# Penalties applied to every self-attention tile by GpSimd, two heads at a time, in a decoder layer

## The chip, the cores and the metric

The kernel runs on one core of a Trainium2 chip. The metric is the device time of one execution in microseconds (us); three executions of the kernel before took 903.59, 895.02 and 897.58 us, median 897.58. The engines are PE (TensorE, matrix products), DVE (VectorE), ACT (ScalarE), POOL (GpSimd) and SP, which issues most of the DMAs. Each engine works through its own list of instructions in order; semaphores tie the lists together.

## The reference, cut to what matters

Four batches of 512 positions with 256 features pass through gated self-attention, cross-attention (both 16 heads of 16 dimensions), and a quantised feed-forward block, each with a residual and a LayerNorm.

```
g = sigmoid(x @ Wg + bg);  Zi = g (row), Zj = g (column)
res   = (1-Zi)*max(1-Zi-Zj, 0) + Zi*min(1-Zi+Zj, 1)
scope = clip((s-2)**(1-g) + 2 - |i-j|, 1e-32, 1)
log_pen = log(max(res*scope, 1e-32))           # 512 x 512 per batch, the same for all heads
scores  = q k^T / 4 + log_pen                  # self-attention
probs   = softmax(scores);  ctx = probs @ v
cross:  probs = softmax(q k^T / 4 + mask * -1e9)
```

Adding log_pen ahead of the exponential is the same as multiplying the exponential by the penalty. A softmax allows any shift per row, as long as nothing overflows or vanishes.

## The kernel before, in words

The attention part is cut into 32 groups of four heads: 16 self groups (4 batches x 4), 16 cross groups. In order: self 0; self 1, cross 0; self 2, cross 1; self 3, cross 2; cross 3, with four groups each, numbered 0 to 31 (self groups are 0 to 7, 12 to 15 and 20 to 23). A group has 16 tiles of 128 x 512 scores.

A **step** has 16 slots and works on three groups at once. In slot i of step n, PE makes the score tile i+2 of group n for its row maxima (`max_tile`, L1400, rows are queries) and the transposed score tile i of group n-2 for its exponentials (`exp_tile`, L1420, rows are keys); DVE takes a row maximum (`row_max`, L921); ACT takes an exponential (`exponential`, L813); and PE multiplies finished probabilities with V (`context`, L1445), four heads per instruction group, in two halves per key tile. "s1,2" below is the step whose maxima are those of self-attention of batch 1, group 2; "c" is cross. The maxima become an extra set of rows of the query stack: DVE splits them in three bf16 parts (`shift_part`, L905 to L911, slots 0 and 1), PE turns them (`m`, slot 5), ACT copies and stores them; the product with them then subtracts the maximum. At the step's end all this moves on by one group.

Between these, slots carry **jobs** from a table written by hand (`make_plan`): projections `q`, `k` (PE L1303, two copies on ACT L726, then on POOL `rest` L655, on ACT `middle` L732, on POOL `low` L660), `v`, the gates (`gate`, `gates`, `diagonals`, `reach`), the penalties (`pen`, DVE, seven instructions for each of four 128 x 512 tiles, L978 to L990), residual and LayerNorm jobs, output projection, and the weights of the feed-forward (`wprep`). DVE runs the jobs of a slot two slots late (`DVE_LAG`), POOL one slot late (`POOL_LAG`).

How far one engine may run ahead is set by buffers: two PSUM banks for maxima, three for exponentials, two for jobs, and `NP` = 8 probability tiles. In slot i, `max_tile` waits until the maximum two tiles back is taken, and `exp_tile` until the exponential three tiles back is done. What stands behind a waiting instruction on its engine waits too.

**Penalties before.** ACT makes the logarithm of all four penalty tiles (`ln`, L756, which changes ACT's function table twice). DVE's row maximum adds it (`lp`) to the scores. For the transposed tiles there are two ways by key tile (kt). For kt 1 and 3 the logarithm is turned by PE and kept in two f16 parts, and PE adds both to the scores by products with an identity (L1424, L1425). For kt 0 and 2 (`MUL_KT`) the penalty itself is turned, and POOL multiplies the exponentials of each head with it (`multiply`, L645, 128 x 512 each).

The context of a key tile is computed in the next key tile's slots (`i % GH >= 2`, kt = i // GH - 1); the last one falls into the next step (slots 1, 2).

## Time and profile before

| | |
|---|---|
| times of three runs | 903.59, 895.02, 897.58 us |
| profiled execution | its span is 894.6 us; the page gives no other time for it |
| busy | PE 714.0, DVE 655.1, ACT 483.9, POOL 290.8 us |
| steps with exponentials of self groups | 93.5 to 300.9, 382.0 to 482.2 and 561.4 to 665.2 us |
| last context of the attention | 795.8 us; the feed-forward follows |

The profile shows for each instruction when it ran and what ended the engine's idle time before it. A DVE or POOL instruction that is held up after it was started is shown longer, not as idle: the duration holds the wait. A matmul's duration holds the passage through the array, so its cost in a dense row is read from the distance of two starts. The limits of a step are taken where ACT copies the context of its group (L792), so "the step of group n" runs from the copy of group n-1 to that of group n.

### The profile page before, as it was taken

The page shows a single profiled execution, that of the slowest core. Times are in us where ns is not written, and L with a number is a line of the kernel's source. Part 1 is how long each engine was busy: PE and PEld are TensorE (multiplying, and loading weights), DVE is VectorE, ACT ScalarE, POOL GpSimd, SP SyncE. Part 2 cuts the span into 40 slices and gives each one's busy share as a digit, 9 for nine tenths or more (in the row PEclk, how much of TensorE's full clock was granted, in tenths as well). Part 3 has the DMA queues.
Part 4 walks back from the last instruction along what each step waited for, and adds up shares of the span by engine and source line. Part 5 has one row for each costly group of instructions (what it writes and reads, how often), then busy time and mean ns, then how long its engine had stood idle before and what let it go on. Part 6 is the DMA issues. An engine that isn't in the chain of part 4 may idle for free.

```text
span 894.6 us, 12845 instructions
## 1 busy us (share of the span) xinstructions
PE 714.0 (80%) x4374; PEld 281.8 (31%) x4374; DVE 655.1 (73%) x1704; ACT 483.9 (54%) x800; POOL 290.8 (33%) x257
## 2 busy tenths in 40 slices
PE   5156878998778889999898899997788699974754
PEld 3033222443223233444232333442222134332221
DVE  5956794676589777688995666689787477717996
ACT  2312446554445767745456677445456476863634
POOL 4202554544445313235463022455223000001314
PEclk9587899999889999999899999999899799996965
DMA  2662111110221313302222123134111411000002
GB/s 69 172 169 86 38 56 56 56 50 14 73 62 56 92 38 103 88 18 62 61 57 77 52 59 93 42 86 111 56 37 39 100 51 32 6 1 1 0 1 94
DMA packets 34896, 54.00 MB, mean 60 GB/s; under 512 B 4368, under 2 KB 25872, under 8 KB 34832
## 3 DMA queue, kind: packets, MB, share of 16 engines
q1 hardware_dynamic: 32912, 51.61, 20.1%
q10 hardware_dynamic: 1920, 1.57, 1.1%
q8 instruction: 36, 0.59, 0.3%
q14 instruction: 28, 0.23, 0.1%
HBM read 36.91 MB, written 14.68 MB: 58 GB/s over the span
## 4 chain that ended last, share of the span: by engine, by line
PE 43%; DVE 28%; ACT 8%; POOL 7%; issue 6%; DMA 4%; SPq 3%; ACTq 0%; POOLq 0%; DVEq 0%
PE ps L1445 9%; DVE unused L921 9%; PE ps L1400 8%; PE ps L1420 6%; PE ps L1387 5%; PE ps L1303 4%; POOL probs L645 3%; PE ps L1380 2%; ACT probs L813 2%; PE ps L1424 2%; PE ps L1425 2%; DMA xT<-in_xT 2%; POOL rest L655 2%; DMA KS<-parts_kc 2%; DVE x L958 1%
## 5 line engine op out<-in xcount | busy, mean ns | idle before, releaser
L1400 PE MATMUL ps<-KS,QS 96*128 96x512 bf16 x512 | 205.1, 402 | 91.4 <-DVE mx L921 62.2
L813 ACT ACTIVATE probs<-ps 128x512 f32<-128x512 f32 x256 | 149.3, 596 | 167.3 <-PE ps L1425 107.7
L645 POOL TENSOR_TENSOR probs<-probs,penT 128x512 f32<-128x512 f32 x128 | 165.4, 1310 | 205.4 <-ACT probs L813 205.2
L921 DVE CUSTOM_DVE_ANT_0 unused<-ps,lp 128x512 bf16<-128x512 f32 x256 | 171.1, 685 | 77.1 <-PE ps L1400 73.0
L1420 PE MATMUL ps<-QS,KS 108*128 108x512 bf16 x512 | 199.5, 393 | 7.1 <-ACT probs L813 7.0
L813 ACT ACTIVATE probs<-ps,mask_col 128x512 f32<-128x512 f32 x256 | 166.4, 687 | 58.0 <-PE ps L1420 56.6
L921 DVE CUSTOM_DVE_ANT_0 unused<-ps,mask_rest 128x512 bf16<-128x512 f32 x192 | 128.9, 684 | 45.5 <-PE ps L1400 44.1
L1400 PEld LDWEIGHTS ps<-KS,QS 96*128 96x128 bf16 x512 | 50.7, 99 | 242.9 <-DVE mx L921 144.4
L655 POOL TENSOR_TENSOR rest<-proj,parts 128x512 f32<-128x512 f32 x32 | 39.0, 1218 | 169.3 <-ACT parts L726 168.7
L1445 PE MATMUL ps<-probs,v_s 128*32 128x256 f32 x1024 | 84.5, 403 | 5.6 <-POOL probs L645 4.8
L1445 PE MATMUL ps<-probs,v_c 128*32 128x256 f32 x1024 | 82.9, 397 | 0.6 <-ACT probs L813 0.6
L1420 PEld LDWEIGHTS ps<-QS,KS 108*128 108x128 bf16 x512 | 50.6, 100 | 44.6 <-ACT probs L813 18.4
L627 POOL TENSOR_SCALAR rstd<-mv 128x4 f32<-128x4 f32 x12 | 2.7, 225 | 152.9 <-DVE mv L949 152.9
L921 DVE CUSTOM_DVE_ANT_0 unused<-ps,mask_row 128x512 bf16<-128x512 f32 x64 | 43.4, 682 | 12.2 <-PE ps L1400 12.1
L1424 PE MATMUL ps<-lpT_hi,ident_h 128*128 128x512 f16 x128 | 51.6, 403 | 0.0
L1425 PE MATMUL ps<-lpT_lo,ident_h 128*128 128x512 f16 x128 | 51.3, 400 | 0.0
L660 POOL TENSOR_TENSOR parts<-rest,parts 128x512 bf16<-128x512 f32 x32 | 38.5, 1203 | 19.0 <-ACT parts L732 19.0
L921 DVE DVE_READ_ACCUMULATOR2_ANT mx<- 128x1 f32 x512 | 41.6, 81 | 0.0
L1445 PEld LDWEIGHTS ps<-probs,v_s 128*32 128x32 f32 x1024 | 20.7, 109 | 62.6 <-issue 57.8
L732 ACT ACTIVATE parts<-rest 128x512 bf16<-128x512 f32 x32 | 20.2, 631 | 31.5 <-POOL rest L655 30.8
L1445 PEld LDWEIGHTS ps<-probs,v_c 128*32 128x32 f32 x1024 | 20.5, 108 | 52.9 <-issue 50.2
L726 ACT ACTIVATE proj<-ps,bias_qk 128x512 f32<-128x512 f32 x32 | 22.0, 686 | 26.7 <-PE ps L1303 26.0
(185 smaller groups left out, 964.6 us busy)
## 6 DMA issues: line engine op xcount, KB each, us to landing
parts_qs<-parts SPq DMA_DIRECT2D x8, 384.0 KB, 2.6
parts_ks<-parts SPq DMA_DIRECT2D x8, 384.0 KB, 2.7
QS<-parts_qs SPq DMA_DIRECT2D x16, 192.0 KB
KS<-parts_ks SPq DMA_DIRECT2D x16, 192.0 KB
parts_kc<-parts SPq DMA_DIRECT2D x8, 384.0 KB, 2.5
parts_qc<-parts SPq DMA_DIRECT2D x8, 384.0 KB, 2.7
QS<-parts_qc SPq DMA_DIRECT2D x16, 192.0 KB
KS<-parts_kc SPq DMA_DIRECT2D x16, 192.0 KB
```

Source lines behind the costliest of these rows:

```text
L645: g.tensor_tensor(probs[:, T % NP, :], probs[:, T % NP, :], penT[:, MUL_KT.index(kt), :], ALU.mult)\
L655: g.tensor_tensor(rest[:, :], proj[:, w % 2, :], parts[:, w % 2, 0, :], ALU.subtract)\
L660: g.tensor_tensor(parts[:, w % 2, 2, :], rest[:, :], parts[:, w % 2, 1, :], ALU.subtract)\
L813: s_.activation(probs[:, T % NP, :], ps[:, EXP_BANKS[T % 3], :], ACT.Exp, bias=bias)\
L921: v.tensor_tensor_reduce(out=unused[:, i % 2, :], in0=ps[:, MAX_BANKS[i % 2], :], in1=lp[:, t, :] if kind == "s" else mask_row(b), scale=1 ...
L1303: ins = mm(bank(u), W[what + kind][:, k, c * P:(c + 1) * P], src[:, k, :], start=k == 0, stop=k == HC - 1)
L1387: ins = mm(bank(u)[:, tt * H:(tt + 1) * H], src[:, k, (2 * i + tt) * P:(2 * i + tt + 1) * P], w[:, k, :], start=k == 0, stop=k == HC - 1)
L1400: mm(ps[:, MAX_BANKS[i % 2], :], QS[0:SK, slot, j, t * P:(t + 1) * P], KS[0:SK, slot, j, :], start=True, stop=True).then_inc(max_scores, 1)
L1420: ins = mm(o, KS[0:SM, slot, j, kt * P:(kt + 1) * P], QS[0:SM, slot, j, :], start=True, stop=not logged)
L1424: mm(o, ident_h[:, :], lpT_hi[:, k, :], start=False, stop=False)
L1425: ins = mm(o, ident_h[:, :], lpT_lo[:, k, :], start=False, stop=True)
L1445: ins = mm(ps[VC * j:VC * (j + 1), PV_BANK, q], V[kind][:, kt, GH * g + j, :], probs[:, (T + j) % NP, q], start=kt == 0 and half == 0, sto ...
```

## The change

All penalties become multiplications. POOL multiplies the exponentials of all four key tiles, and takes two heads (two neighbouring probability tiles, 128 x 1024) per instruction, after every odd slot. The logarithm, its f16 parts and PE's two additions go. The row maximum of self tiles has no second input now (`tensor_reduce`), so it is the unpenalised one; 40 is taken off it (added to its negative) so that heavily penalised rows keep their precision. `NP` is 12, and the context of a key tile is computed two key tiles later; the last two fall into the next step (slots 0, 1 and 4, 5), for cross groups also. `oT` and `norm` move from slots 2 and 4 to 5 and 7. The penalties of batch 0 move from the prologue into step s0,0, and their turning to step s0,1, ahead of the gates of batch 1.

```diff
-MUL_KT = (0, 2)
+HEADROOM = 40.0
-NP = 8
+NP = 12
         if s.norm is not None:
-            at = [(1, ("last_context", s.norm, 0)), (2, ("last_context", s.norm, 1)), (2, ("oT", s.norm)),
-                  (4, ("norm", s.norm))] + list(at)
+            at = [(0, ("late_context", s.norm, NT - 2, 0)), (1, ("late_context", s.norm, NT - 2, 1)),
+                  (4, ("late_context", s.norm, NT - 1, 0)), (5, ("late_context", s.norm, NT - 1, 1)),
+                  (5, ("oT", s.norm)), (7, ("norm", s.norm))] + list(at)
...
-        tasks=[(1, 4, ("v", "s", 0)), (6, 15, ("lpB", 0))])
-    add(("s", 0, 1), stacks=[], at=[(15, ("mask_col",))], tasks=[(0, 5, ("gate", 1)), (4, 15, ("q", "s", 1)), (7, 15, ("pens", 1, (0,)))])
+        tasks=[(1, 4, ("v", "s", 0)), (0, 13, ("pens", 0, range(NT)))])
+    add(("s", 0, 1), stacks=[], at=[(15, ("mask_col",))], tasks=[(0, 3, ("penT", 0)), (4, 9, ("gate", 1)), (6, 15, ("q", "s", 1)), (11, 15, ("pens", 1, (0,)))])
...
-    add(("s", 0, 3), at=[(14, ("ln", 1))], tasks=[(0, 13, ("pens", 1, (3,)))])
+    add(("s", 0, 3), tasks=[(0, 13, ("pens", 1, (3,)))])
...
-    + expand(("pens", 0, range(NT))) + [("ln", 0), ("own_rows",)]
+    + [("own_rows",)]
...
             def multiply(n, i):
                 T = TG * n + i
                 kt = i // GH
...
                 pool.wait_ge(exp_done, T + 1)
-                g.tensor_tensor(probs[:, T % NP, :], probs[:, T % NP, :], penT[:, MUL_KT.index(kt), :], ALU.mult)\
+                two = probs[:, (T - 1) % NP:(T - 1) % NP + 2, :]
+                g.tensor_tensor(two, two, penT[:, kt, :].unsqueeze(1).broadcast_to((P, 2, S)), ALU.mult)\
                     .then_inc(pen_applied, 1)
...
-                if s is not None and s.p2 is not None and groups[s.p2][0] == "s" and i // GH in MUL_KT:
+                if s is not None and s.p2 is not None and groups[s.p2][0] == "s" and i % 2:
                     multiply(s.p2, i)
...
             def shift_part(n, k):
-                m = mx[:, n % 2, :, :]
+                m, room = mx[:, n % 2, :, :], HEADROOM if groups[n][0] == "s" else 0.0
                 if k == 0:
-                    leave(v.tensor_scalar(mparts[:, :, 0, :], m, -1.0, None, ALU.mult))
+                    leave(v.tensor_scalar(mparts[:, :, 0, :], m, -1.0, room, ALU.mult, ALU.add))
...
             def row_max(n, i):
-                v.tensor_tensor_reduce(out=unused[:, i % 2, :], in0=ps[:, MAX_BANKS[i % 2], :],
-                                       in1=lp[:, t, :] if kind == "s" else mask_row(b),
+                if kind == "s":
+                    v.tensor_reduce(mx[:, n % 2, t, j:j + 1], ps[:, MAX_BANKS[i % 2], :], AX.X, ALU.max)\
+                        .then_inc(max_done, 1)
...
             def exp_tile(n, i):
-                ins = mm(o, KS[0:SM, slot, j, kt * P:(kt + 1) * P], QS[0:SM, slot, j, :],
-                         start=True, stop=not logged)
-                if logged:
-                    k = log_kt.index(kt)
-                    mm(o, ident_h[:, :], lpT_hi[:, k, :], start=False, stop=False)
-                    ins = mm(o, ident_h[:, :], lpT_lo[:, k, :], start=False, stop=True)
-                ins.then_inc(exp_scores, 1)
+                mm(ps[:, EXP_BANKS[T % 3], :], KS[0:SM, slot, j, kt * P:(kt + 1) * P], QS[0:SM, slot, j, :],
+                   start=True, stop=True).then_inc(exp_scores, 1)
...
-                        if i % GH >= 2 and i > GH:
-                            context(s.p2, i // GH - 1, i % GH - 2)
+                        if i % GH < 2 and i >= 2 * GH:
+                            context(s.p2, i // GH - 2, i % GH)
```

On POOL, the first self step with exponentials (s0,2) reads before as follows; L655 and L660 are the two POOL instructions of a `k` projection.

```order
L660 TENSOR_TENSOR parts<-rest,parts 128x512
L645 TENSOR_TENSOR probs<-probs,penT 128x512 x3
L655 TENSOR_TENSOR rest<-proj,parts 128x512
L645 TENSOR_TENSOR probs<-probs,penT 128x512
L660 TENSOR_TENSOR parts<-rest,parts 128x512
```

With the change the same place has twice as much multiplied between them (L633 is `multiply`, L643 and L648 are `rest` and `low`):

```order
L633 TENSOR_TENSOR probs<-probs,penT 128x1024
L643 TENSOR_TENSOR rest<-proj,parts 128x512
L633 TENSOR_TENSOR probs<-probs,penT 128x1024 x2
L648 TENSOR_TENSOR parts<-rest,parts 128x512
L633 TENSOR_TENSOR probs<-probs,penT 128x1024
```

The instructions are as many as before (eight a step), each over 1024 elements, spread evenly over the slots where they had come in bursts of four, and `rest` stands directly behind one.

On PE, the slots of a logged key tile (here in step s1,1) read before:

```order
L1400 MATMUL ps<-KS,QS 128x512
L1420 MATMUL ps<-QS,KS 128x512
L1424 MATMUL ps<-lpT_hi,ident_h 128x512
L1425 MATMUL ps<-lpT_lo,ident_h 128x512
L1445 MATMUL ps<-probs,v_s 32x256 x4
```

and in the change (L1363 for maxima, L1378 for exponentials, L1398 for contexts, L1343 the turning of a penalty tile):

```order
L1363 MATMUL ps<-KS,QS 128x512
L1378 MATMUL ps<-QS,KS 128x512
L1398 MATMUL ps<-probs,v_s 32x256 x4
L1343 MATMUL ps<-ident_f,pen 128x128 x4
L1363 MATMUL ps<-KS,QS 128x512
L1378 MATMUL ps<-QS,KS 128x512
L1398 MATMUL ps<-probs,v_s 32x256 x4
```

The two products with the identity are gone in eight of 16 slots; nothing takes their place on PE.

On DVE, the start of the program before, from `reach` on:

```order
L1057 TENSOR_SCALAR reach<-reach 128x4
L978 TENSOR_SCALAR pen_a<-z_row,w_col 128x512
L980 TENSOR_SCALAR pen_a<-pen_a,w_col 128x512
L982 TENSOR_SCALAR pen_b<-z_row,w_col 128x512
L984 SCALAR_TENSOR_TENSOR pen_a<-pen_b,z_col,pen_a 128x512
L986 TENSOR_SCALAR pen_b<-neg_abs,reach 128x512
L988 SCALAR_TENSOR_TENSOR pen_a<-pen_b,pen_a 128x512
L990 TENSOR_SCALAR pen<-pen_a 128x512
```

and in the change (L1034 is `own_rows`, L894 the row maximum, L952 to L964 the penalties, L1064 the bias of `v`):

```order
L1031 TENSOR_SCALAR reach<-reach 128x4
L1034 COPY KS<-own_rows 32x4x4x512
L1125 MEMSET amax 128x18
L894 TENSOR_REDUCE mx<-ps 128x1 x3
L952 TENSOR_SCALAR pen_rows<-pen_rows,w_col 128x512
L954 TENSOR_SCALAR pen_rows<-pen_rows,w_col 128x512
L894 TENSOR_REDUCE mx<-ps 128x1
L1064 TENSOR_TENSOR v_s<-ps,bias_vs 128x32x16
L956 TENSOR_SCALAR pen_rows<-pen_rows,w_col 128x512
```

The 28 penalty instructions of batch 0 stood ahead of the first row maximum; now two of them stand behind each of the first row maxima.

## Rows read from the trace of the kernel before

**Rows 1.** The page: busy us, share of the span, instructions of each engine.

```profile
PE 714.0 (80%) x4374; PEld 281.8 (31%) x4374; DVE 655.1 (73%) x1704; ACT 483.9 (54%) x800; POOL 290.8 (33%) x257
```

**Rows 2.** The page: the chain that ended last, by line.

```profile
PE ps L1445 9%; DVE unused L921 9%; PE ps L1400 8%; PE ps L1420 6%; PE ps L1387 5%; PE ps L1303 4%; POOL probs L645 3%; PE ps L1380 2%; ACT probs L813 2%; PE ps L1424 2%; PE ps L1425 2%; DMA xT<-in_xT 2%; POOL rest L655 2%; DMA KS<-parts_kc 2%; DVE x L958 1%
```

**Rows 3.** Windows over steps: start:end, length, busy by engine, PEclk, DMA share, GB/s.

```profile
93.50:120.40 26.90, 22.93 (x126) 7.06 (x124) 22.36 (x51) 14.19 (x26) 17.31 (x14) 0.92 0.16 49
248.40:300.90 52.50, 43.62 (x256) 14.69 (x256) 47.95 (x111) 25.39 (x45) 26.04 (x20) 0.93 0.23 61
429.50:455.40 25.90, 21.54 (x123) 7.04 (x124) 23.83 (x57) 10.52 (x20) 11.34 (x9) 0.87 0.21 54
120.40:147.60 27.20, 21.46 (x128) 7.20 (x129) 19.65 (x52) 15.88 (x23) 11.61 (x9) 0.94 0.14 44
382.00:406.70 24.70, 23.68 (x147) 10.40 (x148) 19.77 (x51) 12.03 (x23) 9.93 (x8) 0.95 0.12 30
455.40:482.20 26.80, 23.87 (x134) 8.00 (x134) 18.96 (x49) 14.86 (x27) 13.27 (x12) 0.94 0.23 68
607.20:665.20 58.00, 43.64 (x271) 14.54 (x272) 48.70 (x130) 27.57 (x47) 22.30 (x19) 0.91 0.25 64
147.60:248.40 100.80, 87.84 (x564) 36.23 (x562) 64.04 (x178) 50.23 (x93) 49.21 (x42) 0.97 0.18 51
406.70:429.50 22.80, 20.62 (x136) 8.73 (x136) 18.86 (x50) 10.35 (x19) 10.82 (x11) 1.00 0.22 58
561.40:607.20 45.80, 42.94 (x283) 19.11 (x282) 34.69 (x90) 21.57 (x38) 22.02 (x19) 1.00 0.26 64
248.40:274.70 26.30, 20.93 (x123) 6.96 (x124) 23.89 (x56) 10.48 (x19) 11.96 (x9) 0.87 0.21 55
```

**Rows 4.** Groups by line: shapes, count | busy us, mean ns | idle before.

```profile
L645 POOL TENSOR_TENSOR probs<-probs,penT 128x512 f32<-128x512 f32 x128 | 165.4, 1310 | 205.4 <-ACT probs L813 205.2
L1210 DVE TENSOR_REDUCE amax<-h_all 128x1 f32<-128x1024 f32 x10 | 12.0, 1201 | 0.0
L756 ACT ACTIVATE lp<-pen 128x2048 f32<-128x2048 f32 x4 | 7.6, 1910 | 5.7 <-DVE pen L990 5.7
L756 ACT ACT_TABLE_LOAD x4 | 5.1, 1283 | 0.2
```

**Rows 5.** Timeline near 233 us, PE: start, length, then the instruction.

```profile
233.21 0.38 PE L1420 MATMUL ps<-QS,KS 108*128 108x512 bf16 x1
233.43 0.38 PE L1424 MATMUL ps<-lpT_hi,ident_h 128*128 128x512 f16 x1
```

**Rows 6.** Timeline: DVE beside POOL, and DVE with POOL idle.

```profile
28.58 1.15 POOL L655 TENSOR_TENSOR rest<-proj,parts 128x512 f32<-128x512 f32 x1
28.75 1.26 DVE L982 TENSOR_SCALAR pen_b<-z_row,w_col 128x512 f32<-128x512 f32 x1
...
33.31 0.49 DVE L978 TENSOR_SCALAR pen_a<-z_row,w_col 128x512 f32<-128x512 f32 x1
...
36.91 0.43 DVE L990 TENSOR_SCALAR pen<-pen_a 128x512 f32<-128x512 f32 x1
...
317.35 2.36 POOL L669 TENSOR_TENSOR x<-x,bias_o 128x1024 f32<-128x1024 f32 x1
```

**Rows 7.** The same view, DVE in that place.

```profile
317.54 2.21 DVE L911 TENSOR_TENSOR mparts<-mrest,mparts 128x16 bf16<-128x16 f32 x1
```

**Rows 8.** Timeline of the start.

```profile
39.51 1.01 PE L1400 MATMUL ps<-KS,QS 96*128 96x512 bf16 x2 [16.41 <-DMA KS<-parts_ks]
41.85 0.67 DVE L921 CUSTOM_DVE_ANT_0 unused<-ps,lp 128x512 bf16<-128x512 f32 x1
42.44 0.08 DVE L921 DVE_READ_ACCUMULATOR2_ANT mx<- 128x1 f32 x1
70.12 0.56 PE L1319 MATMUL ps<-wg,xT 128*128 128x1 f32 x2 [7.93 <-DMA xT<-in_xT]
91.08 0.63 PE L1420 MATMUL ps<-QS,KS 108*128 108x512 bf16 x1
```

More of the change, by code:

```diff
@@ L82, in expand @@
         return [("pen", rest[0], t, k) for t in rest[1] for k in range(PEN_OPS)]
-    if what == "lpB":
-        return [("lpB", *rest, kt) for kt in range(NT)]
+    if what == "penT":
+        return [("penT", *rest, kt) for kt in range(NT)]
     if what == "residual":
@@ L281, in decoder_layer @@
         parts = sb("parts", [P, 2, PARTS, S], BF16, att)
-        z_row = sb("z_row", [P, S], F32, att)
+        pen_rows = sb("pen_rows", [P, 3, S], F32, att)
+        z_row, pen_a, pen_b = (pen_rows[:, i, :] for i in range(3))
         z_col = sb("z_col", [P, NT], F32, att)
@@ L422, in norms_of, with key_tiles, penalised @@
             return [unit[("norm", groups.index((kind, b, g)))] for g in range(NG)]
[L424 to L433 removed]
+        def key_tiles(n, kt):
+            return NT * sum(k == "s" for k, _, _ in groups[:n]) + kt + 1
+        def penalised(eng, n, kt):
+            eng.wait_ge(pen_applied, GH // 2 * key_tiles(n, kt))
         slots = [(s, i) for s in steps for i in range(TG)]
@@ L1325, in do @@
                         ins.then_inc(side_full[u % 2], 1)
-                elif what == "lpB":
+                elif what == "penT":
                     b, kt = job[1:]
-                    pe.wait_ge(lp_made, b + 1)
-                    src = pen if kt in MUL_KT else lp
-                    turn(u, [src[:, t, kt * P:(kt + 1) * P] for t in range(NT)])
+                    pe.wait_ge(pen_made, b + 1)
+                    turn(u, [pen[:, t, kt * P:(kt + 1) * P] for t in range(NT)])
                 elif what == "x1T":
@@ L1349, in do @@
                     ins.then_inc(side_full[u % 2], 1)
-                elif what == "last_context":
-                    context(job[1], NT - 1, job[2])
+                elif what == "late_context":
+                    context(*job[1:])
                 elif what == "norm":
@@ L1439, in context @@
                 T = TG * n + GH * kt
[L1440 to L1441 removed]
+                if kind == "s":
+                    penalised(pe, n, kt)
                 else:
```

124 lines of the change are left out of this document (39 added, 85 removed).

## The prediction

> **What bounds the kernel now.** I read the busy times first, then the chain of waits, then the stretches of steps, last the timeline. No engine is full: PE 80%, DVE 73%, ACT 54%, POOL 33% [rows 1]. The chain changes engines all the time, and the lines that the change removes (L1424, L1425) hold 4% of it, 36 us, POOL's multiplications 3% [rows 2]. So the bound is the lockstep of a slot, and each step must be read alone. Sixteen steps carry exponentials of self groups; together they take 411.4 us [rows 3]: 105.3 in the four that also carry 13 to 15 penalty instructions (s0,2; c0,0; c0,1; c1,0), 78.7 in the three with about seven (s0,3; s2,2; c1,1), 58.0 in the two with weight preparation, 169.4 in the seven others. In a step full of penalties DVE is busy 23.9 of 26.3 us; in the seven others it is busy 117.6 of 169.4, and PE sets the pace (151.4 of 169.4) [rows 3].
>
> **How DVE and POOL meet.** A penalty instruction takes 0.49 us with POOL idle, and 1.26 beside a POOL instruction of 1.15 us: it ends 0.28 after that one [rows 6]. A 16-element DVE instruction begun 0.19 us after POOL's 128 x 1024 addition took 2.21 us and ended with it [rows 6, 7]. So DVE is held to the end of the POOL instruction. The Trainium skill's "SBUF — State Buffer" (Who interferes with whom) says why: a DVE instruction with two SBUF inputs, or in a mode with two ports, shares a port pair with GpSimd, and the later one blocks for the other's whole instruction. The trace agrees with 2.21 us, and this speaks against longer GpSimd instructions. By a rule of shared bandwidth, the wait wouldn't grow with POOL's length and the forecast would be the first rival below.
>
> **The parts.**
> PE: a logged tile loses two matmuls that start 0.22 us apart [rows 5]: 8 slots x 2 x 0.22 = 3.5 us a step, 56 us in 16 steps, all on PE. It is a gain only where PE sets the pace.
>
> POOL: eight instructions per step as before, of 2.36 instead of 1.31 us (165.4 in all [rows 4, 6]), so 18.9 us a step instead of 10.5. The Trainium skill's "GPSIMD Engine Reference" (Instruction dispatch) gives 2.5 cycles per element as the floor with two inputs, an estimate of 2.13 us at its 1.2 GHz; the four additions of this shape took 2.36, so I keep the row. By the page a step would hold 1.8 us less. With a `q` or `k` projection come four instructions of some 1.2 us (4.8), and what DVE holds POOL up, about 0.3 each time. So 19 to 24 us is a floor: against 24.2 us, the mean of the seven others (169.4 / 7), it takes most of PE's gain.
>
> DVE, row maxima: from start to the reading of the maximum 0.59 us [rows 8]. A reduction over 1024 elements took 1.20 [rows 4]; half of that is 0.60, at most 0.67 if a fixed part of 0.13 stays. I take no change; the ends are -0.02 and +0.08 on 256 of them, -5 to +20 us if all were on the path, which they aren't. The penalties: seven instructions from 33.31 to 37.34 us without POOL, 4.03, or 0.58 each [rows 6].
>
> A step full of penalties, now: 17 maxima x 0.6 = 10.2, 15 penalties x 0.58 = 8.7, shift parts and normalisation 1.6: 20.5; DVE was busy 23.9, so waits hold 3.4 us, 0.4 per multiplication. Changed, the multiplications are evenly spread, one in two slots. After a held penalty instruction comes a maximum (0.6), and the next penalty instruction meets the next multiplication at about that age: a wait of 2.36 - 0.65 = 1.7 us. Lower end 0.8 (0.4 x 2.36 / 1.31, rounded up), upper end 2.21 [rows 7]. I take seven of eight hits at 1.7: 11.9. Then the step is 20.5 + 11.9 = 32.4 us, and DVE's former idle time (26.3 - 23.9 = 2.4, behind the logged tiles) is gone. That is +6.1 on the mean of 26.3, +24 for four steps. By 0.8 it is 20.5 + 6.4 = 26.9 (+2 for four), by 2.21 x 8 it is 38.2 (+48).
>
> Steps with seven: one such instruction per two slots, so two slots need POOL's 2.36 + 0.5: 22.9, plus 4.8 in c1,1. s0,3 comes to 24 (27.2 before, with the wait for the logarithm), s2,2 with its gates to 27, c1,1 to 27.7: 78.7, no change.
> Weight steps: three short instructions per slot after a maximum; some three to four more waits a step are longer by 1.05 (2.36 - 1.31), 7 us for both, less 2 for PE: +5.
> The seven others: PE -3.5 each (-24) as the most; back come shift parts (four per step, each held now up to 2.2 instead of 1.2: about +1.5), ACT's `middle` behind `rest` behind a longer multiplication (+1.2 for each of four jobs), together 15, and POOL's floor, for which I count 5: -4.
> The logarithm: four times 1.91 and four table loads of 1.28 [rows 4], as many table loads back. In s0,3 it is counted; in c0,3 and c1,3 some 4.5 us of ACT go, which had room; -2 each: -4.
>
> The start: before, the penalties lay under the DMA that lets PE start at 39.51, and DVE's first maximum was at 41.85 behind the copy of `own_rows` [rows 8]. Now that copy is early (and may hold POOL's first `rest` by a us), the first maximum comes at 40 to 41, but step s0,0 has 28 penalties: 16 x 0.6 + 28 x 0.58 + 1.4 for `v` = 27.2, to 68. Before, PE got past the gates of batch 1 only at 70.12, when xT landed, at slot 0 of the next step. Now their turn is at slot 4, so the DMA is covered, but if it came later, its delay would show as before. Four slots with penalty turnings bring us to 73, then 12 slots of 1.3 us give 89; the first exponential was at 91.08. I count 0, with -3 and +4 as ends.
> The later context costs one more key tile behind the last exponential, about 1 us; twelve probability tiles cover the two key tiles of delay, about 8 slots; without them the context would wait for POOL each time.
>
> **Sum:** +24 + 0 + 5 - 4 - 4 + 0 + 1 = +22 us. Against the profiled execution (span 894.6; it has no other time) that is 917; the median of the runs is 3 above that span, 897.6, so 919 to 920. I forecast **919 us**.
>
> **Rivals.**
> *A, PE's gain shows.* The waits stay below some 0.7 us per multiplication, since penalties slip in ahead of POOL's start. The point is 26.3 = 20.5 + 8 x 0.72. Then full steps cost 0 (or -1), three steps -3 each, weights -4, seven others -2.5 each (POOL's floor), logarithm -4: -35, 863; between it and no change 880. For it: POOL idled 205.4 us before its multiplications [rows 4], the chain counts 36 us for the products. Against: rows 6 and 7. Chance 0.22.
> *B, they cancel.* Waits near 1.1: full steps +2.7 each, the rest -11: 0, 897. Chance 0.18.
> *C, the forecast.* 906 to 932. Chance 0.42.
> *D, POOL becomes the bound.* Row maxima, shift parts and `middle` all stand behind POOL's backlog; the four shift parts wait 2.2 each in a step, and PE, with two banks ahead, stands with DVE. Three us more in each of ten steps: 949. For it: POOL at 24 plus holds of 2 to 4 us in steps with a projection, above the 24.2 us of the seven others. Against: a delay of two key tiles absorbs bursts. It decides as soon as POOL has no gap of 1 us left in a step. Chance 0.18.
>
> About 1% is what these runs can tell from no change (895.0 to 903.6 for one kernel). Faster by over 1% is A, 0.22; within 1% B, 0.18; slower C and D, 0.60. The range of 8 in 10 is 876 to 944: it leaves out the better half of A and the worse half of D. C's own is 906 to 932.
>
> **What would show it.** Right: multiplications of 2.36 to 2.6 us, 128 of them, 300 us or more of POOL; penalty instructions of 1.2 to 1.6 us in the mean in full steps, where it is (8.7 + 3.4) / 15 = 0.8 now; steps c0,0 and c1,0 of 31 to 34 us; DVE busy above 690 us in all; PE's idle time ahead of the score tiles for the maxima ended by DVE. PE busy falls by some 50 us in any case. A lower granted clock than 0.87 in the full steps would make them longer still. Wrong: full steps below 28 us (A), or all self steps at 27 and more with POOL busy 90% (D), or a first exponential later than 95 us, where I count nothing.

## The result, and the profile after

| | before | after |
|---|---|---|
| median | 900.59 us (4 runs, 895.02 to 907.12) | 951.39 us (4 runs, 950.12 to 957.26) |
| ratio | | 1.0585, 95% interval 1.0518 to 1.0653 |
| span of the profiled execution | 894.6 | 955.5 |

The change costs 51 us by the medians. The profiled execution after took 957.26, the slowest of its four, so that the two profiles differ by 61 us. Forecast: 919, with 944 as the upper end. The direction was right, the size not.

The page after: busy times, the chain by engine and by line, and the groups that answer to [rows 1, 2, 4].

```profile
PE 719.7 (75%) x4116; PEld 268.3 (28%) x4118; DVE 720.1 (75%) x1440; ACT 465.1 (49%) x788; POOL 427.3 (45%) x256
...
DVE 44%; PE 35%; issue 7%; POOL 6%; ACT 4%; DMA 2%; SPq 1%; ACTq 0%; POOLq 0%; DVEq 0%
PE ps L1398 8%; DVE unused L897 8%; PE ps L1363 7%; DVE mx L894 6%; PE ps L1378 5%; PE ps L1267 5%; PE ps L1350 5%; POOL probs L633 3%; PE ps L1343 2%; DVE pen_rows L962 2%; DVE mparts L880 2%; DVE x L933 1%; DVE pen_rows L956 1%; POOL rest
...
L633 POOL TENSOR_TENSOR probs<-probs,penT 128x1024 f32<-128x1024 f32 x128 | 304.1, 2389 | 151.3 <-ACT probs L787 151.1
L894 DVE TENSOR_REDUCE mx<-ps 128x1 f32<-128x512 f32 x256 | 169.0, 683 | 89.8 <-PE ps L1363 89.1
```

POOL's multiplications went from 165.4 us to 304.1, DVE's busy time from 655.1 to 720.1 although 264 DVE records are gone. POOL's multiplications hold no more than 3% of the chain, as before, but DVE's share went from 28% to 44% (PE's from 43% to 35%): they act through DVE.

The steps that answer to [rows 3], cut where ACT takes the first exponential of a group (start:end, length, busy by engine, PEclk, DMA share, GB/s): c0,0; s2,2; c1,1; the two weight steps; s1,0 to s1,3.

```profile
261.10:292.40 31.30, 24.83 (x108) 5.75 (x112) 31.16 (x50) 10.62 (x18) 20.13 (x9) 0.50 0.21 54
405.60:437.50 31.90, 24.57 (x138) 10.68 (x138) 25.57 (x38) 11.47 (x22) 18.34 (x8) 0.78 0.15 39
494.10:524.90 30.80, 22.86 (x116) 7.28 (x120) 21.63 (x49) 13.18 (x24) 20.39 (x11) 0.78 0.11 29
646.00:717.30 71.30, 48.30 (x244) 14.20 (x248) 63.46 (x126) 27.59 (x46) 41.77 (x20) 0.70 0.20 53
143.30:261.10 117.80, 87.99 (x510) 34.68 (x510) 84.89 (x120) 50.65 (x93) 85.89 (x44) 0.82 0.17 47
```

In c0,0, a step full of penalties, DVE is busy without a gap (31.16 of 31.30). In s1,0 to s1,3 PE, POOL and DVE are each busy 85 to 88 of 117.8 us: none is full, and the time goes in waits for one another. The waits of the changed kernel (us in total, times, longest):

```profile
PE ps L1363 <- DVE mx L894: 66.0, 47, 5.7
PE ps L1363 <- DVE mx L897: 57.4, 52, 4.3
ACT parts L721 <- POOL rest L643: 39.9, 24, 5.2
```

In the kernel before, one line holds the maxima of both kinds, self and cross:

```profile
PE ps L1400 <- DVE mx L921: 62.2, 77, 3.2
ACT parts L732 <- POOL rest L655: 30.8, 22, 2.9
```

PE waits 123.4 us for a row maximum instead of 62.2. What delays DVE shows at the start of the light step s1,1 of the changed kernel; L882, L884 and L886 are shift parts of 16 elements, L894 row maxima:

```profile
168.73 9.26 POOL L633 TENSOR_TENSOR probs<-probs,penT 128x1024 f32<-128x1024 f32 x4
168.84 2.28 DVE L882 SCALAR_TENSOR_TENSOR mrest<-mx,mparts 128x16 f32<-128x16 f32 x1
171.04 0.68 DVE L894 TENSOR_REDUCE mx<-ps 128x1 f32<-128x512 f32 x1
171.64 1.77 DVE L884 TENSOR_SCALAR mparts<-mrest 128x16 bf16<-128x16 f32 x1
171.78 0.39 PE L1363 MATMUL ps<-KS,QS 96*128 96x512 bf16 x1 [1.68 <-DVE mx L894]
173.45 2.26 DVE L886 SCALAR_TENSOR_TENSOR mparts<-mrest,mparts 128x16 bf16<-128x16 f32 x1
175.64 2.07 DVE L894 TENSOR_REDUCE mx<-ps 128x1 f32<-128x512 f32 x3
176.38 0.61 PE L1363 MATMUL ps<-KS,QS 96*128 96x512 bf16 x1 [3.99 <-DVE mx L894]
```

Three instructions of 16 elements take 6.3 us, each to the end of the multiplication beside it; the row maximum between them, whose input is in PSUM, takes its 0.68 beside POOL. PE, two banks ahead, stands 1.68 and then 3.99 us. Its next matmul takes 0.61 instead of 0.39. The granted clock of four stretches, one ahead of these waits, two in them and one behind (columns as above), shows why; 1.00 is 2.4 GHz, 0.50 is 1.2. PE was busy 0.70 of the 6 us in the middle:

```profile
160.00:170.00 10.00, 9.87 (x70) 4.24 (x62) 7.73 (x12) 5.56 (x10) 8.78 (x6) 1.00 0.03 10
170.00:173.00 3.00, 0.70 (x3) 0.11 (x2) 3.00 (x3) 1.18 (x2) 3.00 (x2) 1.00 0.93 241
173.00:176.00 3.00, 0.00 (x0) 0.00 (x0) 2.97 (x3) 0.02 (x1) 3.00 (x3) 0.68 0.27 74
176.00:180.00 4.00, 3.62 (x16) 1.34 (x16) 1.67 (x4) 1.09 (x2) 1.99 (x1) 0.50 0.12 41
```

Two steps later, in s1,3, the same happens through ACT (L643 is `rest`, L721 `middle`, L1019 a gate instruction of four elements, L1084 one for the mask):

```profile
239.05 2.35 POOL L633 TENSOR_TENSOR probs<-probs,penT 128x1024 f32<-128x1024 f32 x1
239.60 2.08 DVE L1084 TENSOR_SCALAR mask_row<-mask_row 128x512 f32<-128x512 f32 x1
241.36 1.33 POOL L643 TENSOR_TENSOR rest<-proj,parts 128x512 f32<-128x512 f32 x1
242.72 0.63 ACT L721 ACTIVATE parts<-rest 128x512 bf16<-128x512 f32 x1 [4.14 <-POOL rest L643]
243.25 2.04 ACT L787 ACTIVATE probs<-ps 128x512 f32<-128x512 f32 x4
243.89 0.61 PE L1378 MATMUL ps<-QS,KS 108*128 108x512 bf16 x1 [2.73 <-ACT probs L787]
250.44 2.05 DVE L1019 TENSOR_SCALAR w_col<-z_col 128x4 f32<-128x4 f32 x1
```

ACT's `middle` waits 4.14 us for `rest`, which stood behind the multiplication; the exponentials stand behind `middle`, and PE 2.73 us behind them.

### The profile page after: what moved, and what is told of

It is laid out like the page before. It is cut to its first block, busy times and chain, and to the rows that moved or that the text cites. A ratio compares the mean times of both kernels' runs of the same rounds, so it can differ in the third digit from the quotient of the medians.

```text
span 955.5 us, 12050 instructions
## 1 busy us (share of the span) xinstructions
PE 719.7 (75%) x4116; PEld 268.3 (28%) x4118; DVE 720.1 (75%) x1440; ACT 465.1 (49%) x788; POOL 427.3 (45%) x256
## 4 chain that ended last, share of the span: by engine, by line
DVE 44%; PE 35%; issue 7%; POOL 6%; ACT 4%; DMA 2%; SPq 1%; ACTq 0%; POOLq 0%; DVEq 0%
PE ps L1398 8%; DVE unused L897 8%; PE ps L1363 7%; DVE mx L894 6%; PE ps L1378 5%; PE ps L1267 5%; PE ps L1350 5%; POOL probs L633 3%; PE ps L1343 2%; DVE pen_rows L962 2%; DVE mparts L880 2%; DVE x L933 1%; DVE pen_rows L956 1%; POOL rest L643 1%; ACT probs L787 1%
## 5 line engine op out<-in xcount | busy, mean ns | idle before, releaser
L633 POOL TENSOR_TENSOR probs<-probs,penT 128x1024 f32<-128x1024 f32 x128 | 304.1, 2389 | 151.3 <-ACT probs L787 151.1
L1363 PE MATMUL ps<-KS,QS 96*128 96x512 bf16 x512 | 224.4, 439 | 148.3 <-DVE mx L894 66.0
L894 DVE TENSOR_REDUCE mx<-ps 128x1 f32<-128x512 f32 x256 | 169.0, 683 | 89.8 <-PE ps L1363 89.1
L1378 PE MATMUL ps<-QS,KS 108*128 108x512 bf16 x512 | 217.6, 429 | 4.7 <-ACT probs L787 4.6
L1363 PEld LDWEIGHTS ps<-KS,QS 96*128 96x128 bf16 x512 | 52.5, 103 | 320.7 <-DVE mx L897 114.4
L643 POOL TENSOR_TENSOR rest<-proj,parts 128x512 f32<-128x512 f32 x32 | 38.7, 1208 | 151.9 <-ACT parts L715 151.3
L1398 PE MATMUL ps<-probs,v_s 128*32 128x256 f32 x1024 | 103.0, 482 | 0.0
L1398 PE MATMUL ps<-probs,v_c 128*32 128x256 f32 x1024 | 83.9, 402 | 0.3 <-ACT probs L787 0.3
L1378 PEld LDWEIGHTS ps<-QS,KS 108*128 108x128 bf16 x512 | 52.6, 104 | 49.9 <-issue 26.0
L648 POOL TENSOR_TENSOR parts<-rest,parts 128x512 bf16<-128x512 f32 x32 | 37.7, 1179 | 14.8 <-ACT parts L721 14.8
L1398 PEld LDWEIGHTS ps<-probs,v_s 128*32 128x32 f32 x1024 | 22.4, 120 | 74.6 <-issue 69.1
L721 ACT ACTIVATE parts<-rest 128x512 bf16<-128x512 f32 x32 | 20.2, 630 | 40.9 <-POOL rest L643 39.9
L1398 PEld LDWEIGHTS ps<-probs,v_c 128*32 128x32 f32 x1024 | 20.6, 109 | 54.0 <-issue 50.7
L698 ACT ACTIVATE penT<-ps 128x512 f32<-128x512 f32 x16 | 9.6, 603 | 51.6 <-PE ps L1343 42.8
L933 DVE TENSOR_SCALAR x<-x,mv,rstd 128x256 f32<-128x256 f32 x32 | 24.4, 785 | 5.8 <-POOL rstd L615 5.8
L1468 PE MATMUL ps<-downT,h_int 128*128 128x256 bf16 x96 | 19.9, 353 | 11.3 <-DVE h_int L1202 7.2
```

Of the source, the lines that this page charges most:

```text
L633: g.tensor_tensor(two, two, penT[:, kt, :].unsqueeze(1).broadcast_to((P, 2, S)), ALU.mult)\
L643: g.tensor_tensor(rest[:, :], proj[:, w % 2, :], parts[:, w % 2, 0, :], ALU.subtract)\
L648: g.tensor_tensor(parts[:, w % 2, 2, :], rest[:, :], parts[:, w % 2, 1, :], ALU.subtract)\
L894: v.tensor_reduce(mx[:, n % 2, t, j:j + 1], ps[:, MAX_BANKS[i % 2], :], AX.X, ALU.max)\
L933: ins = v.tensor_scalar(dst, src, mv[:, k, t, 0:1], rstd[:, k, t:t + 1], ALU.subtract, ALU.mult)
L1363: mm(ps[:, MAX_BANKS[i % 2], :], QS[0:SK, slot, j, t * P:(t + 1) * P], KS[0:SK, slot, j, :], start=True, stop=True).then_inc(max_scores, 1)
```

## The experiments

All ratios are to the kernel before on the same chip, with 95% intervals; its median was 897.8 to 900.0 us in them, so times from different experiments compare to a few us. The expectations use four names. By the *lock theory* a DVE instruction is held to the end of the POOL instruction beside it, and PE waits with DVE. By the *length theory* the cost follows the length of one POOL instruction; by the *total-time* (or occupancy) *theory* it follows POOL's busy time. The *price* of POOL's work is the time by which the kernel gets shorter when that work is left out. "..." marks lines of an edit that are left out.

### What POOL's multiplications are worth

e1 and e17 leave nearly all of the multiplications out, e11 half of each (half the columns of the self probabilities stay unpenalised).

```diff
# e1, from the changed kernel (e11: S // 2 in place of 8)
-                two = probs[:, (T - 1) % NP:(T - 1) % NP + 2, :]
+                two = probs[:, (T - 1) % NP:(T - 1) % NP + 2, 0:8]
...
# e17, from the kernel before
-                g.tensor_tensor(probs[:, T % NP, :], probs[:, T % NP, :], penT[:, MUL_KT.index(kt), :], ALU.mult)\
+                g.tensor_tensor(probs[:, T % NP, 0:16], probs[:, T % NP, 0:16], penT[:, MUL_KT.index(kt), 0:16], ALU.mult)\
```

**e1.** 

> The changed kernel, with POOL multiplying only 8 of 512 columns per head (the rest of the penalties is left out); the number and place of the 128 POOL instructions, and all waits, stay. Lock theory (DVE is held to the end of POOL's 2.39 us instructions, and PE with it): the 90 us or so of extra DVE time and the stalls behind it go, 951 falls to 850 to 875 us, DVE busy from 720 to below 640, the granted clock of the full steps back to 0.9 and more. Theory of the order (the later contexts, the plan with penalties in the first step, or the plain row maxima are what costs): the time stays above 920.

Measured: 811.11 us, 0.9005 [0.8952, 0.9058]. The multiplications cost 140 us (951.4 - 811.1), more than any theory gave them.

**e11.** 

> The changed kernel with POOL multiplying the first 256 of 512 columns of each head (half of the penalties is left out): 128 instructions of about 1.2 us, the length and the total of the kernel before, spread as in the changed kernel. With 16 elements per instruction the time was 811, with 1024 it is 951. Lock theory: what a held DVE instruction waits is POOL's length less 0.65 us, so 0.55 instead of 1.7; a third of the 140 us is left: 845 to 865 us. If the cost followed POOL's total busy time in proportion: 881.

Measured: 860.69, 0.9548 [0.9501, 0.9595]. 128 instructions of 1.31 us cost 50 us (860.7 - 811.1), as the lock theory had it.

**e17.** 

> The kernel before, GpSimd multiplying 16 of the 512 columns of each of its 128 tiles (the rest of those exponentials stay unpenalised). In the changed kernel 331 us of one-head multiplications cost 110 us of time and 150 us cost 50, a third of GpSimd's busy time each. By that price the 153 us of the kernel before cost 50: 843 to 855. If its multiplications lie beside work of TensorE, which is its bound: 885 to 897. What is left between this kernel and the 811 of the changed one with next to no multiplication is what the removed logarithms, identity products and the other maximum bring: 39 us by the first theory, some 80 by the second.

Measured: 842.83, 0.9392 [0.9362, 0.9422]. So the first theory holds: in the kernel before, the 128 multiplications cost 57 us (899.4 - 842.8), though PE was the busiest engine. The busy times of e17 and of e1, and their multiplications:

```profile
PE 702.2 (83%) x4372; PEld 281.5 (33%) x4374; DVE 602.5 (71%) x1704; ACT 483.3 (57%) x800; POOL 154.5 (18%) x257
L645 POOL TENSOR_TENSOR probs<-probs,penT 128x16 f32<-128x16 f32 x128 | 30.0, 234 | 287.0 <-ACT probs L813 286.9
```
```profile
PE 657.8 (81%) x4118; PEld 260.7 (32%) x4118; DVE 583.7 (72%) x1440; ACT 462.7 (57%) x788; POOL 155.3 (19%) x256
L633 POOL TENSOR_TENSOR probs<-probs,penT 128x16 f32<-128x16 f32 x128 | 32.1, 250 | 262.2 <-ACT probs L787 262.2
```

Without the multiplications DVE is busy 53 us less in the kernel before and 136 us less in the changed one, with the same DVE instructions: that much of its busy time was waiting. ACT is not slowed by them: an exponential of a self tile takes 596 ns before and after.

### The length of one POOL instruction

```diff
# e2, from the changed kernel: one head per instruction
-                two = probs[:, (T - 1) % NP:(T - 1) % NP + 2, :]
-                g.tensor_tensor(two, two, penT[:, kt, :].unsqueeze(1).broadcast_to((P, 2, S)), ALU.mult)\
+                g.tensor_tensor(probs[:, T % NP, :], probs[:, T % NP, :], penT[:, kt, :], ALU.mult)\
...
# e16 (changed kernel), e13 (before, with MUL_KT.index(kt)): half a head per instruction
+                for lo in (0, S // 2):
+                    one = probs[:, T % NP, lo:lo + S // 2]
+                    ins = g.tensor_tensor(one, one, penT[:, kt, lo:lo + S // 2], ALU.mult)
...
# e12, from the kernel before: two heads per instruction, for key tiles 0 and 2 as before
+                two = probs[:, (T - 1) % NP:(T - 1) % NP + 2, :]
+                g.tensor_tensor(two, two, penT[:, MUL_KT.index(kt), :].unsqueeze(1).broadcast_to((P, 2, S)), ALU.mult)\
```

**e2.** 

> The changed kernel with one head per POOL instruction again (256 of 128 x 512, after every slot), everything else as changed. POOL's total work is the same within 5% (about 315 us). Lock theory by length: a DVE instruction is held 1.2 us at most instead of 2.35, the shift parts lose about 1 us each, and POOL's rest of a projection comes 1.2 us earlier: 925 to 940 us. Theory of occupancy (what counts is how much of a step POOL works, not the length of one instruction; a row of held DVE instructions meets twice as many POOL instructions): 948 to 965 us.

Measured: 920.96, 1.0233 [1.0174, 1.0291]: 30 us less than two heads. That is the length theory's direction, and a little more than its range of 925 to 940.

**e12.** 

> The kernel before with two heads per POOL instruction on its two multiplied key tiles (64 of 128 x 1024 instead of 128 of 128 x 512), nothing else changed: POOL's total is 10% less, only the length of one instruction doubles. Lock theory by length: in the full steps four waits of 1.7 instead of eight of 0.4 us, shift parts held 2.2 instead of 1.2, contexts later: 1.010 to 1.025 (908 to 922 us). If only POOL's total counts: 0.990 to 1.000.

Measured: 931.66, 1.0353 [1.0306, 1.04], slower than either theory: the same elements in half as many instructions, 32 us more. DVE is busy 673.7 us, 19 more; PE waits longer for maxima and for the products:

```profile
PE ps L1401 <- DVE mx L922: 77.0, 77, 4.2
...
PE ps L1446 <- POOL probs L646: 9.9, 9, 1.7
```

The second was 4.8 us before. So the later multiplications themselves cost about 5 of the 32, and the wait for maxima 15; the rest isn't assigned.

**e13.** 

> The kernel before, with each multiplication of one head by GpSimd (128x512, 1.2 us) cut into two of 128x256; same work, half the length of one instruction. If the length of one GpSimd instruction sets the holds, and by the straight line through one head and two (897 and 932 here): 16 us less, 875 to 888. If only GpSimd's total time counts: 897 or, with the start of 128 more instructions of some 0.06 us, up to 905. If the later arrival of a multiplication at the context products was what cost the 32 us of two heads per instruction: 893 to 900.

Measured: 891.34, 0.9915 [0.9881, 0.9949]: 8 us less, where the straight line gave 16. This lies in none of the three ranges.

**e16.** 

> The changed kernel with pieces of 128x256: same work for GpSimd, a quarter of the length of one instruction. Two heads took 951, one head 921, next to no work 811. If the cost were proportional to the length of one instruction, it would be some 35 above 811 for a quarter, 846 to 870. If the length carries the 30 us between two heads and one and the time that GpSimd is busy carries the rest, 903 to 911. If the number of instructions costs more than their length gives back: 921 or more.

Measured: 925.26, 1.0295 [1.025, 1.0341]. Nothing is gained over one head; both theories with a length in them fail below 1.3 us, and the third, with 921 or more, holds. The pages of e2 and of e16 show one reason:

```profile
PE 701.9 (77%) x4118; PEld 265.1 (29%) x4118; DVE 682.4 (75%) x1440; ACT 464.9 (51%) x788; POOL 453.9 (50%) x384
...
L632 POOL TENSOR_TENSOR probs<-probs,penT 128x512 f32<-128x512 f32 x256 | 331.3, 1319 | 88.4 <-ACT probs L786 87.7
```
```profile
PE 709.1 (77%) x4116; PEld 270.6 (29%) x4118; DVE 655.5 (71%) x1440; ACT 464.2 (50%) x788; POOL 495.2 (54%) x640
...
L634 POOL TENSOR_TENSOR probs<-probs,penT 128x256 f32<-128x256 f32 x512 | 374.1, 766 | 63.7 <-ACT probs L791 63.7
```

DVE is busy 27 us less, but POOL 41 us more. The other reason is in one place of e16's timeline:

```profile
170.57 9.60 POOL L634 TENSOR_TENSOR probs<-probs,penT 128x256 f32<-128x256 f32 x14
171.57 8.64 DVE L884 TENSOR_SCALAR mparts<-mx 128x16 bf16<-128x16 f32 x1
181.07 0.61 PE L1367 MATMUL ps<-KS,QS 96*128 96x512 bf16 x1 [7.73 <-DVE mx L898]
```

A 16-element instruction stands not for one POOL instruction but for the whole run of them, 8.64 us, and PE for 7.73.

### Keeping short DVE work away from POOL

```diff
# e4: penalties of batches 2 and 3 in steps without multiplications (likewise for b + 1)
-    add(("c", 0, 0), fetch=[("cT", 1)], tasks=[(0, 15, ("pens", 2, (0, 1)))])
+    add(("c", 0, 0), fetch=[("cT", 1)])
-    add(("c", 0, 2), tasks=[(0, 10, ("k", "s", 2)), (8, 15, ("residual", 1))])
+    add(("c", 0, 2), tasks=[(0, 10, ("k", "s", 2)), (8, 15, ("residual", 1)), (0, 13, ("pens", 2, (0,)))])
...
# e5: the shift parts leave DVE's list and are made on POOL, in the slot of the fourth part
+                if job[0] == "shift" and job[2] == 3:
+                    shift_parts(job[1])
...
# e6: POOL's jobs of a slot ahead of its multiplication
+                if late is not None:
+                    for job in late.items[at]:
+                        do(job)
                 if s is not None and s.p2 is not None and groups[s.p2][0] == "s" and i % 2:
                     multiply(s.p2, i)
```

**e4.** 

> The changed kernel, with the penalties of batches 2 and 3 moved from the steps in which POOL multiplies (s2,2; c0,0; c0,1; c1,0; c1,1) to those in which it does not (one tile each in c0,2; c0,3; s2,0; s2,1 and c1,2; c1,3; s3,0; s3,1); possible only because the row maxima no longer need the logarithm. Lock theory: the five steps lose 4 to 9 us each (56 penalty instructions no longer meet the multiplications, 0.58 us each and 1.2 to 1.7 of wait in half of them), the eight get 4 us of DVE work of which half is covered by its idle time: 951 - 35 + 12 = 915 to 930 us. If the moved work costs the same wherever it stands: 945 to 955.

Measured: 935.25, 1.04 [1.0337, 1.0464]. This lies between the two forecasts. c0,0 falls from 31.3 to 18.4 us and c1,0 from 29.4 to 21.3, but the shift parts, which stay, grow from 67.6 to 89.9 us in sum (in the four full steps from 12.2 to 18.3): the waits move on in part to what is left. Where the penalties now stand, outside the 16 self steps, the profile is 20.7 us longer.

**e5.** 

> The changed kernel, with the splitting of the maxima in three bf16 parts (four DVE instructions a step, 67.6 us in all in the changed kernel, 24 with POOL's work taken away) done by five small POOL instructions in POOL's own order. POOL, being one queue, never waits for its own port. Lock theory, with the shift parts as the largest share of what was missed in the light steps: all 16 self steps lose 3 to 4 us of DVE time, two thirds of it on the path: 915 to 930 us. Theory that the light steps grew by ACT's wait for POOL (rest before middle) or by the lower clock: 945 to 955, or slower, since POOL gets 1.5 us more a step.

Measured: 935.15, 1.0406 [1.037, 1.0443], 16 us less than the changed kernel and between the two forecasts. But not all self steps share in it. By the profiles (23 us apart) the full steps get 6.8 us shorter, those with seven penalties 9.3, the weight steps 2.8 and the rest of the program 8.3; the seven other steps, where 23.5 us of shift parts left DVE, get 4.5 longer. PE waits 20.0 us for maxima there instead of 29.7, but POOL is busy 149.7 instead of 140.8 and ACT waits 12.6 us for `rest` instead of 8.8. So in these light steps POOL's queue took back what DVE gained.

**e6.** 

> The changed kernel, with POOL's jobs of a slot (the rest and low parts of projections, the inverse deviations) ahead of the multiplication of the next slot instead of behind it. ACT waited 39.9 us for rest in the changed kernel (30.8 before), up to 5.2 in one piece. If these waits cost in the six self steps with a projection: 12 projections halves x 1 to 2 us less, 930 to 940 us. Lock theory alone (DVE decides, ACT has room): 946 to 953.

Measured: 949.12, 1.0566 [1.0524, 1.0608]. ACT's wait for `rest` falls from 39.9 to 29.1 us, the time by 2: POOL's own order is worth next to nothing.

**e7** is e2 and e4 together. 

> One head per POOL instruction and the penalties of batches 2 and 3 in the steps without multiplications, both at once (each alone: ratio 1.023 and 1.040 to the kernel before, the changed kernel 1.0585). If they act on the same waits, the gain is less than the sum: 1.010 to 1.020 (907 to 916 us); if on different ones, 1.005 (902).

Measured: 907.6, 1.0103 [1.0068, 1.0137], at the lower end of the range for the same waits.

**e9** is e2, e4 and e5 together. 

> The changed kernel with one head per POOL instruction, penalties of batches 2 and 3 in the steps without multiplications, and the shift parts on POOL: the first two together gave a ratio of 1.010 to the kernel before, the third alone took 0.018 off. If the third still acts: 0.995 to 1.000 (893 to 898 us). If POOL, with 317 us of multiplications and 25 of shift parts, is now the bound in self steps: 1.010 or slower.

Measured: 904.86, 1.0055 [1.0018, 1.0092], between the two forecasts: the third edit takes 0.005 off here, where alone it took 0.018.

**e14** is e16 and e4 together. 

> The changed kernel with the multiplications in pieces of 128x256 and the penalties of batches 2 and 3 made in steps without multiplications. With pieces of 128x512 it took 908. Length theory: 890 to 898. Total-time theory: 908 to 915.

Measured: 932.3, 1.036 [1.0324, 1.0397], 25 us slower than e7 and outside of both theories. In its trace four shift parts are held for 9.1 to 11.0 us under runs of 14 to 17 pieces. One such place there is in e7, with pieces of 1.2 us:

```profile
269.63 11.05 POOL L632 TENSOR_TENSOR probs<-probs,penT 128x512 f32<-128x512 f32 x9
...
272.12 8.60 DVE L879 TENSOR_SCALAR mparts<-mx 128x16 bf16<-128x16 f32 x1
...
281.59 0.61 PE L1362 MATMUL ps<-KS,QS 96*128 96x512 bf16 x1 [5.23 <-DVE mx L896]
```

**e10** is e5's edit in the kernel before. 

> The kernel before, with only the splitting of the maxima moved from DVE (44.4 us in all, 24 of it work) to POOL (28% to 33% busy there). Lock theory: the four small instructions a step are the ones that stand ahead of row maxima and meet POOL; without them self steps lose 1 to 2 us, cross steps 0.5: 0.970 to 0.985 (873 to 887 us). If PE sets the pace of the kernel before: 0.995 to 1.000.

Measured: 894.22, 0.9913 [0.9875, 0.995], 0.9% under the kernel before and between the two forecasts. The interval is clear of 1, though the gain is no larger than the scatter of single runs.

**e15** adds e13's pieces to e10. 

> The kernel before with both: multiplications in pieces of 128x256 and the shift's parts made by GpSimd (which alone gave 0.991). Length theory: 0.97 to 0.985, 870 to 886, the fastest that does all the work. Total-time theory: 0.99 to 1.00.

Measured: 901.99, 1.0028 [1.0003, 1.0054]. The two gains of 0.9% don't add; together they are none. The total-time theory is the nearer.

### The clock, and the balance of the two ways

```diff
# e3, from the changed kernel: PE makes score tiles of key tiles 1 and 3 three times
+                for _ in range(3 if kind == "s" and kt in (1, 3) else 1):
...
# e8, from the kernel before: maxima without the logarithm, e4's places, ln in a later step
+                if kind == "s":
+                    v.tensor_reduce(mx[:, n % 2, t, j:j + 1], ps[:, MAX_BANKS[i % 2], :], AX.X, ALU.max)\
...
# e18, from the kernel before
-MUL_KT = (0, 2)
+MUL_KT = (0,)
```

**e3.** 

> The changed kernel, where every score product for exponentials of key tiles 1 and 3 of self groups is done three times over into the same bank (same result): PE gets back the 256 short matmuls that the change took away, 3.5 us a step at full clock. Clock theory (taking work from PE let the granted clock fall to 0.5 to 0.8 in the self steps, which doubles the rest of PE's work there): no slower, 935 to 955 us, granted clock of the full steps higher than in the changed kernel. Lock theory alone: PE is not the bound in the full steps, it is in the light ones: 955 to 975. If PE sets the pace throughout: 951 + 56 = 1007.

Measured: 966.34, 1.075 [1.068, 1.0819]. The granted clock rose from 0.82 to 0.87 in the mean, and in c0,0 from 0.50 to 0.77, where the step went from 31.3 to 30.3 us. The four full steps together went from 120.3 to 118.3 us, with more work for PE in them: there the lower clock costs little. In the seven other steps the repeated products hardly raised it (0.87 to 0.89 in the mean), and what it costs there this run doesn't tell. PE is busy 14 us more there in the changed kernel than in e1, with the same matmuls (144.3 against 130.3): an estimate of the most that the clock can cost.

**e8.** 

> The kernel before with one part of the change: row maxima without penalties (10 added to the negative maximum, beside its factor 2^43 in the penalties), so that penalties and logarithm are needed only by the exponentials; POOL still multiplies two of four key tiles, one head per instruction, and PE adds the logarithm for the others. The penalties of batches 2 and 3 are moved to the steps without multiplications, those of batch 1 spread over four steps. Lock theory: five full steps lose 3 to 5 us each, eight quiet ones gain 1 to 1.5: 880 to 890 us. If the moved work costs the same anywhere: 895 to 902.

Measured: 905.53, 1.0062 [1.003, 1.0093]. The steps with penalties get 12.7 us shorter (the full ones 8.4), but the seven others 8.6 longer and the steps outside these, where penalties and logarithm now stand, 12.5. Both theories miss it: what the moved work gave back in one place it cost in another.

**e18.** 

> The kernel before with only key tile 0 multiplied by GpSimd and the three others added as logarithms by TensorE: 64 multiplications fewer, 64 pairs of identity products more, the other way than the change goes. At a third of GpSimd's busy time the multiplications removed give 25 us back; the identity products cost 64 x 0.43 = 27 us where TensorE is the bound. GpSimd as price alone: 872 to 880. Both: 893 to 905. TensorE as bound alone: 915 to 925.

Measured: 892.35, 0.991 [0.987, 0.995]: a little better than the two prices together. The opposite direction of the change is a gain, of 7 us, again no larger than the scatter of single runs.

## Why the prediction was wrong

The steps of the profiled executions, grouped as in the prediction, cut at each group's first exponential (before's differ by a few us from [rows 3], which cut at the context's copy); "no mult." are e17 and e1:

| | before | before, no mult. | after, no mult. | after | forecast | measured |
|---|---|---|---|---|---|---|
| four full steps | 101.5 | 81.9 | 76.7 | 120.3 | +24 | +18.8 |
| three with seven | 75.1 | 66.6 | 57.1 | 86.1 | 0 | +11.0 |
| weight steps | 59.0 | 46.0 | 46.1 | 71.3 | +5 | +12.3 |
| seven others | 172.8 | 160.7 | 145.0 | 187.8 | -4 | +15.0 |
| all else | 486.3 | 489.8 | 488.5 | 489.9 | -3 | +3.6 |

The forecasts add up to 22 us and the measured column to 61, 10 more than the medians give, since the profile after is of the slowest run. The profile's lines of four of the light steps, s1,0 to s1,3, in the kernel before, e17, e1, e2 and e5, in this order (the changed kernel's stands above):

```profile
141.80:246.20 104.40, 91.51 (x571) 37.44 (x569) 64.86 (x184) 51.40 (x94) 50.27 (x42) 0.95 0.17 49
136.60:233.40 96.80, 90.97 (x571) 37.52 (x569) 57.84 (x184) 51.82 (x95) 17.39 (x42) 0.95 0.19 54
129.90:219.10 89.20, 77.29 (x510) 32.18 (x514) 55.18 (x120) 50.75 (x93) 17.82 (x43) 0.94 0.22 62
142.70:255.50 112.80, 91.12 (x510) 35.39 (x514) 73.59 (x120) 50.93 (x94) 91.14 (x75) 0.80 0.18 49
141.50:262.70 121.20, 93.71 (x510) 37.66 (x514) 70.20 (x104) 50.93 (x94) 91.75 (x64) 0.78 0.16 46
```

**How DVE and POOL meet** was right. The full steps were forecast at +24 us and came to +18.8. DVE is busy 39 us more in them than in e1, 1.2 per multiplication, where I took 1.5; before it was 17.6 more than in e17, 0.55, where I took 0.4. In time the multiplications cost 43.6 us there instead of 19.6, 24.0 more, as forecast; the rest of the change gave 5.2 back, which I had put at nothing. Penalty instructions take 1.21 us there in the mean, inside the 1.2 to 1.6 forecast, and 21 of 57 more than 1.5. c0,0 took 31.3 us and c1,0 29.4 (forecast 31 to 34 for both). By the rule of the Trainium skill's "SBUF — State Buffer" (Who interferes with whom) that was weighed there, the later instruction waits for the other's whole instruction; the holds of 2.26 and 2.28 us agree, those of 8.6 us go further.

**The step that failed is the light steps**: "The seven others", "Steps with seven" and "Weight steps", 1 us in the forecast and 38 measured. There I took PE or POOL's floor as the pace, and POOL's old multiplications as free. e17 shows they were not: they cost 33.6 us of these twelve steps (8.5 with seven penalties, 13.0 with weights, 12.1 in the seven others). The changed ones cost 97.0 (29.0, 25.2, 42.8). In the seven others all that isn't multiplication gained 15.7 us, where I had 24 for PE alone, and 30.7 came back, not 20.

The shift parts in the seven others I had right (12.9 to 23.5 us, forecast +10.5). What I hadn't is that PE, which I took as the pace, waits for the maxima: 5.1 us in these seven steps before and 29.7 after, with a lower granted clock, 0.94 to 1.00 in six of the seven before and 0.70 to 0.93 in six of them after. The holds of the shift parts alone don't explain it, as e5 shows. POOL's amount of work counts there more than the length of its instructions: over e1's 145.0 us, half the work costs 10.6 (e11), all of it in single heads 34.4 (e2), in quarters of the length 46.6 (e16) and in pairs 42.8. How the 42.8 us divide between holds of DVE, ACT's wait for POOL and the clock stays open.

In the steps with seven penalties I reckoned with one per two slots behind POOL and nothing else; they took 1.35 us each in the mean instead of 0.89, and a gate instruction of s2,2 (`w_col`) 2.2 us. s0,3 came out (23.4 us, forecast 24), s2,2 and c1,1 did not (31.9 and 30.8, forecast 27 and 27.7). A POOL floor was a bound from below that I used as the value.

**The sum by mechanism**, from medians: PE's and ACT's work taken away, with all else that isn't multiplication (the later contexts, the plan, the plain maxima), -32 (842.8 to 811.1); twice the multiplications at one head per instruction, 110 instead of 57, +53; two heads per instruction +30 (e2). Together +51; these are differences along one chain of kernels, so they add up by construction. The price of one 128 x 512 multiplication (the time above e17 or e1, by their number) is 0.38 to 0.45 us in the five kernels with instructions of 0.8 to 1.3 us (e13, e11, e2, before, e16), and 0.55 and 0.69 in the two with 2.4 us (after, e12). That this looks like my 0.4 per multiplication is chance: mine was DVE's wait in full steps. And the price isn't even: in the kernel before it is 0.61 us of time in the full steps, 0.35 in those with seven penalties, 0.81 in the weight steps and 0.22 in the seven others; after, per tile, 0.68, 0.60, 0.79 and 0.38.

**The other steps.** PE busy was to fall by 50 us in any case; it is 720 instead of 714. Without the multiplications it does fall by 44 (e17 to e1, 702.2 to 657.8); with them it is 62 higher than in e1, at a granted clock of 0.823 instead of 0.906. The logarithm's -4 outside s0,3 came (c0,3 and c1,3: -5.2). The four steps of cross 3, which the later context reaches, take 3.8 us more (3.3 between e17 and e1), where I had 1; that it is the context isn't shown by a run. The start moved by 0.3 us (91.8 to 91.5).

**The rivals.** A's point was passed by far (1.2 us per multiplication against 0.7); B's 1.1 was nearly met in the full steps, but the others didn't cancel (and its own sum slips: 20.5 + 8 x 1.1 is 3.0 us above 26.3, not 2.7). D gave the time (949) and named the parts that move, shift parts and `middle`, but its sign, POOL without a gap of 1 us in a step, was met in one of the 16 steps only (s3,2): POOL is busy 85.9 of 117.8 us in s1,0 to s1,3, and its order doesn't matter (e6). So its time was met in part by luck, though the amount of POOL's work does count in the light steps. The 30 us of length are not later products: neither in the changed kernel nor in e2 does PE wait anywhere for a multiplied tile. PE's wait for maxima is 26.9 us shorter in e2 (96.5 against 123.4) and DVE's busy time 37.7.

## What to carry to other kernels

Don't take an engine's work as free because another engine is busier: run the kernel once with that work cut to a few columns (e17) before forecasting what its doubling costs. Where GpSimd works beside VectorE, weigh a tile's worth of GpSimd work by its price in the time (here 0.4 us of 1.3 at one head in the mean, 0.2 to 0.8 by the kind of step) and not by its gaps, don't let one instruction grow beyond the 1.3 us of one head, and look for VectorE instructions of a few elements that last as long as GpSimd's. Shorter instructions still gained 0.9% where GpSimd was busy 35% of the span (e13), and nothing where it was busy 39% (e15) or half (e16, e14). After moving work off VectorE, look step by step whether the queue that took it has become the wait (e5).
